# Cross attention on 97 rows: queries and keys laid out by head, column tiles for the rests, maxima among the output jobs

## The chip, the core and the metric

One NeuronCore of a Trainium2 chip. The metric is the device time of one execution in microseconds (us); lower is better. PE is TensorE, DVE is VectorE, ACT is ScalarE, POOL is GpSimd, SP is SyncE, which here only issues DMAs.

## What is computed

A decoder layer over x of [2, 2048, 512] with a context of [2, 154, 512], all in float32:

```python
x = x + linear_attention(layernorm(x))   # 16 heads of 32, elu+1 features of width 128
x = x + cross_attention(layernorm(x), ctx)
x = x + moe(layernorm(x))                # 8 experts, top 6, and a shared expert

def cross_attention(query, ctx):
    q, k, v = (proj(query, Wq, bq), proj(ctx, Wk, bk), proj(ctx, Wv, bv))   # 16 heads of 32
    scores = einsum('bhqd,bhkd->bhqk', q, k) / sqrt(32)
    attn = softmax(scores, axis=-1)                                        # over 154 keys
    return merge(einsum('bhqk,bhkd->bhqd', attn, v)) @ Wo.T + bo
```

## The kernel before

Four stages run one after another, each with its own buffers: `project`, `attend_linear`, `attend_cross` and `experts`. The 4096 tokens are cut into 8 blocks of 512 (`TB`), four a batch. Every engine has its own program; semaphores join them, and each waits in its own order, written out by hand. Products are made exact by splitting a float32 number into a high part (HI, rounded to fp32r) and a low part (LO), and adding three products, HI by HI, HI by LO and LO by HI (`PASSES`).

**`attend_linear`** works on two blocks at once: the heads of block i+1 (`heads`, `attend_group`) are laid between the output jobs of block i (`out_proj`, `transposes`, and XQ, the projection of the queries for cross attention). Four PSUM banks rotate over the jobs in the order of `JOBS`; a bank may be written again when DVE has read the job that had it (`dve_read`). At a block's end PE does XQ 0, the last group of the next heads, XQ 1 and 2, the spreads R 0 to 3 of the reciprocals (`spread_out`), and XQ 3. DVE copies each XQ with its bias to `xq` (L814), an SBUF tile for the whole block, and SP stores it to `xq_dram` with one DMA (L635) when the last is there. Ahead of that store in SP's queue stand the three loads of `q3` for the block after next (L605), for all blocks but the last two. ACT copies the next numerators after normalisation (`normalised`, L680).

**`attend_cross`** loads that block (`load_xq`, L1070), splits it on ACT and DVE (`split_xq`), and holds queries as [128 features, 512 tokens] per group of four heads. The keys `k_w` are masked: the key tile of a head is 128 rows of which 32 are not zero. Scores are made transposed, keys on the partitions: 128 keys of a head are one unit, and the remaining 26 keys of the four heads of a group are a fifth unit, so 20 units a block. A unit is three passes (L1375) and a fourth (L1380) that subtracts each query's maximum:

```python
for c, (s, m) in enumerate(PASSES):
    nc.tensor.matmul(s_bank[n % SBANKS][:], k_w[:, s, g, j * P:(j + 1) * P], q[:, m, g], start=(c == 0), stop=False)
nc.tensor.matmul(s_bank[n % SBANKS][:], minus[:, n // SU, n % SU], mxt[:], start=False, stop=True).then_inc(s_full, 1)
```

ACT takes the exponential of a unit from one of two banks to `ring` (L1156). `attend_group` sums values and denominators: four float32 passes of 32 columns for the heads' main keys (L1407, L1398) and one of 128 columns for the rests (L1409, L1400). The maxima of block k+1 come from other passes (`maxima`, L1349 and L1353), HI by HI only, queries on the partitions, reduced by DVE (L1222); they are spread over the score units of block k, and turned by `turn_maxima`. Then come the division (L1279, L1282), the spreads (L1462), the normalisation (L1287, L1163, L1291), the output projection (L1427), the sum with its statistics (L1239 to L1246), the norm (L1252) and the transposes (L1436), copied by DVE (L1259). Here three PSUM banks rotate. The two batches are a loop; at its start PE makes keys and values (L1321, L1326) and DVE masks them.

## Time and profile before

| | us |
|---|---|
| Median of 3 runs | 2907.85 |
| The runs | 2906.36 to 2916.95 |
| Span of the profiled execution | 2905.3 |
| PE busy in it | 2740.4 (94%) |
| DVE, ACT, POOL busy | 1386.4, 830.9, 133.0 |
| Mean granted clock of TensorE (1 is full) | 0.972 |

The span goes from the first to the last instruction. The profiled execution's own time is not recorded apart from its span; the runs beside it differ from the span by 1 us and more. A window row gives the busy time of each engine in a stretch of the span with its number of instructions, then the granted clock, the share of the DMA engines and the rate. In a timeline row stand the start, the length, the engine and line, and what was released by whom. Matmuls overlap one another, so what one costs is read from start to start, not from its length; a float32 pass shows as two instructions.

### The profile page before, as it was taken

Reading aid. Unit: us, or ns where it says so; the run is one execution under the profiler, and the core shown is the slowest. Engines: PE = TensorE matmul, PEld = TensorE weight load, DVE = VectorE, ACT = ScalarE, POOL = GpSimd, SP = SyncE. Lnnn points to the kernel's source line nnn. Section 1 sums busy time; section 2 is a strip of 40 time slices with the busy share of each in tenths; the row PEclk is TensorE's granted clock in tenths of the full one; section 3 lists DMA queues with packets and bytes.
Section 4 is the critical chain, followed back from the end, with each engine's and each line's share of the span. In section 5 each row is a group of like instructions: output and inputs, shape, how many; then the busy total and the mean of one; then the engine's idle time right before and its main releaser. Section 6 shows DMA issues by size and latency. Waiting matters only on the chain. (4 is left out here: it accounts for less than half of the span.)

```text
span 2905.3 us, 35331 instructions
## 1 busy us (share of the span) xinstructions
PE 2740.4 (94%) x12752; PEld 1961.9 (68%) x12752; DVE 1386.4 (48%) x2146; ACT 830.9 (29%) x1332; POOL 133.0 (5%) x101
## 2 busy tenths in 40 slices
PE   7999999889999699989997999999998999999999
PEld 5666666536556455455555888888886888888887
DVE  4444444368777455465645333333345433433333
ACT  3333333365553133223222111111222122111111
POOL 0000000011121011111110000000000000000000
PEclk9999999989999699989998999999999999999999
DMA  5111111174643311121214000000014000100001
GB/s 171 44 43 43 43 43 29 44 189 128 168 131 101 106 59 52 44 88 59 87 58 155 24 22 22 22 22 22 22 43 174 22 22 22 43 22 22 22 22 58
DMA packets 45023, 182.38 MB, mean 63 GB/s; under 512 B 4496, under 2 KB 6288, under 8 KB 33808
## 3 DMA queue, kind: packets, MB, share of 16 engines
q1 hardware_dynamic: 44656, 180.67, 19.4%
q0 software_dynamic: 288, 0.69, 0.1%
q8 instruction: 45, 0.74, 0.1%
q14 instruction: 34, 0.28, 0.0%
HBM read 123.31 MB, written 58.72 MB: 63 GB/s over the span
## 5 line engine op out<-in xcount | busy, mean ns | idle before, releaser
L1769 PE MATMUL ex_pg<-ex_x,ex_w 128*128 128x512 f32 x3840 | 885.6, 390 | 3.3 <-DVE ex_lt L1652 3.3
L1769 PEld LDWEIGHTS ex_pg<-ex_x,ex_w 128*128 128x128 f32 x3840 | 723.3, 188 | 153.9 <-issue 3.5
L1784 PE MATMUL ex_pd<-ex_w,ex_ht 128*128 128x512 f32 x1920 | 446.6, 389 | 0.0
L1718 DVE TENSOR_TENSOR ex_h<-ex_s_g,ex_pg 128x512 f32<-128x512 f32 x160 | 110.0, 688 | 648.8 <-PE ex_pg L1769 647.9
L1784 PEld LDWEIGHTS ex_pd<-ex_w,ex_ht 128*128 128x128 f32 x1920 | 360.4, 188 | 74.8
L1625 ACT ACTIVATE ex_s_g<-ex_pg 128x512 f32<-128x512 f32 x160 | 95.8, 599 | 748.6 <-PE ex_pg L1769 748.5
L1690 DVE SCALAR_TENSOR_TENSOR ex_acc<-ex_pd,ex_share,ex_acc 128x512 f32<-128x512 f32 x320 | 234.4, 748 | 90.3 <-PE ex_pd L1784 85.5
L450 PE MATMUL pr_pj<-pr_xt,pr_w 128*128 128x512 f32 x768 | 179.6, 395 | 3.1 <-DVE pr_qs L352 1.6
L450 PEld LDWEIGHTS pr_pj<-pr_xt,pr_w 128*128 128x128 f32 x768 | 145.2, 190 | 40.3 <-DVE pr_xt L342 6.8
L366 DVE SCALAR_TENSOR_TENSOR pr_kp<-pr_pk,pr_e 128x512 f32<-128x512 f32 x128 | 87.8, 691 | 142.4 <-ACT pr_e L303 108.1
L1156 ACT ACTIVATE cr_ring<-cr_s_bank 128x512 f32<-128x512 f32 x160 | 95.7, 598 | 202.5 <-PE cr_s_bank L1380 202.5
L1375 PE MATMUL cr_s_bank<-cr_xq,cr_k_w 128*128 128x512 f32 x480 | 151.7, 429 | 0.0
L1222 DVE TENSOR_REDUCE cr_mx<-cr_bank 128x4 f32<-128x512 f32 (+1 forms) x160 | 105.7, 688 | 93.8 <-PE cr_bank L1349 65.7
L1628 ACT CAST ex_ht<-ex_h 128x512 fp32r<-128x512 f32 x160 | 98.6, 616 | 181.4 <-DVE ex_h L1718 181.4
L299 ACT ACTIVATE pr_e<-pr_pk 128x512 f32<-128x512 f32 x128 | 76.4, 597 | 183.2 <-PE pr_pk L462 182.5
L462 PEld LDWEIGHTS pr_pk<-pr_f_w,pr_kt 128*128 128x128 f32 x384 | 64.6, 188 | 88.4 <-issue 72.9
L476 PE MATMUL pr_p_ks<-pr_kp,pr_ones 128*32 128x512 f32 x256 | 123.0, 592 | 0.0
L462 PE MATMUL pr_pk<-pr_f_w,pr_kt 128*128 128x512 f32 x384 | 115.4, 419 | 0.0
L1721 DVE TENSOR_TENSOR ex_ht<-ex_h,ex_ht 128x512 fp32r<-128x512 f32 x160 | 110.3, 689 | 6.8
L1427 PE MATMUL cr_bank<-cr_wo,cr_u 128*128 128x512 f32 x384 | 100.0, 407 | 5.7 <-DVE cr_u L1291 5.7
L850 PE MATMUL li_bank<-li_u_ln,li_wq 128*128 128x512 f32 x384 | 97.2, 407 | 8.4 <-DVE li_u_ln L783 8.4
L1375 PEld LDWEIGHTS cr_s_bank<-cr_xq,cr_k_w 128*128 128x128 f32 x480 | 88.5, 193 | 21.9 <-issue 7.7
(180 smaller groups left out, 2881.5 us busy)
## 6 DMA issues: line engine op xcount, KB each, us to landing
stage<-in_units SPq DMA_DIRECT2D x21, 1536.0 KB, 6.2
li_q<-q_scratch SPq DMA_DIRECT2D x21, 1024.0 KB, 12.1
q_scratch<-pr_qs SPq DMA_DIRECT2D x64, 256.0 KB, 4.0
x_scratch<-cr_x SPq DMA_DIRECT2D x16, 1024.0 KB, 4.3
pr_x<-in_x SPq DMA_DIRECT2D x8, 1024.0 KB, 5.2
li_x<-in_x SPq DMA_DIRECT2D x8, 1024.0 KB, 5.2
x_scratch<-li_x SPq DMA_DIRECT2D x8, 1024.0 KB, 3.9
xq_scratch<-li_xq SPq DMA_DIRECT2D x8, 1024.0 KB, 3.9
```

The costliest lines, as they stand in the source:

```text
L450: mm = nc.tensor.matmul(bank_of(key)[:], stationary(s, c), moving(m, c), start=(n == 0), stop=(n == C * 3 - 1))
L462: mm = nc.tensor.matmul(pk[n % 4][:], kt[:, s, g, t * P:(t + 1) * P], f_w[:, m, g], start=(q == 0), stop=(q == 2))
L476: nc.tensor.matmul(p_ks[g * HD:(g + 1) * HD, :], ones[:], kp[:, n % 4], start=(t == 0), stop=(t == TT - 1), skip_group_check=True).then_in ...
L1222: nc.vector.tensor_reduce(dst, src, AX.X, ALU.max).then_inc(dve_read, 1)
L1375: nc.tensor.matmul(s_bank[n % SBANKS][:], k_w[:, s, g, j * P:(j + 1) * P], q[:, m, g], start=(c == 0), stop=False)
L1427: mm = nc.tensor.matmul(bank_of(k, "O", t)[:], u[:, s, g, t * P:(t + 1) * P], wo[:, m, g], start=(n == 0), stop=(n == 3 * G - 1))
L1628: nc.scalar.copy(ht[:, s % 2, HI, f], h[:, f]).then_inc(ht_hi, 1)
L1690: nc.vector.scalar_tensor_tensor(acc[:, n], pd[t][:], share[:, n, bass.ds(e + s // BLK, 1)], acc[:, n], ALU.mult, ALU.add).then_inc(d_take ...
L1718: nc.vector.tensor_tensor(h[:, f], s_g[:, f], pg[2 * f + 1][:], ALU.mult).then_inc(h_set, 1)
L1721: nc.vector.tensor_tensor(ht[:, s % 2, LO, f], h[:, f], ht[:, s % 2, HI, f].bitcast(F32), ALU.subtract).then_inc(ht_lo, 1)
L1769: mm = nc.tensor.matmul(pg[2 * f + which][:], w[:, slot, sp_, col:col + P], x3[:, m, k, c * TB:(c + 1) * TB], start=(n == 0), stop=(n == 3 ...
L1784: mm = nc.tensor.matmul(pd[t][:], ht[:, s % 2, sp_, f, t * P:(t + 1) * P], w[:, slot, m, WD + f * D:WD + (f + 1) * D], start=(n == 0), sto ...
```

## The change

- In `attend_linear` the copy of XQ splits into HI on ACT (`query`) and LO on DVE; `xq` has two slots, used in turn by the four groups, and each group goes out with its own DMA (HI and LO). The scratch tensor holds both halves.
- In `attend_cross` SP loads queries by head, [32 features x 3, 512 tokens] as HI, LO, HI, one group in three DMAs, into a ring of six slots `q3`. The keys are laid out to match as HI, HI, LO, so one pass over 96 rows gives the sum of the three products. Row 97 of the queries is the maximum of the head, and that of the keys is -1, so that scores and shift are one pass of 97 rows. The rest unit of a group is four passes (`k_rest`), one a head.
- The keys get to that layout by 24 DMAs a batch (`place_keys`). The maxima are computed on 96 rows from all three products, in pieces of 154 keys, three to a bank; they are turned, copied by ACT and brought into row 97 by four DMAs on ACT's queue (`maxima_out`).
- The rests in the sums over values and in the denominators are four passes of 32 columns, column tiles like the main ones. The reciprocals are split into HI and LO, so that the spreads are fp32r.
- The maxima of the next block's first two groups lie among the output jobs of the block before, one at each place, the other two groups among the scores; the output jobs of a block come after the first sum over values of the next. The transposes' copies move to ACT. The batches are written out, and the keys and values of batch 1 stand ahead of the last output jobs of batch 0. The semaphores of this stage are not primed in a block of their own.

```diff
-        xq = sb("xq", [P, G, TB])
+        xq = sb("xq", [P, 2, 2, TB], F32R)
...
-                    sp.wait_ge(dve_read, 2 + job(i, ("XQ", G - 1)))
-                    sp.dma_start(xq_dram[i], xq[:].rearrange("p g t -> p (g t)")).then_inc(xq_out, 16)
+                    for g in range(G):
+                        sp.wait_ge(dve_read, 2 + job(i, ("XQ", g)))
+                        sp.dma_start(xq_dram[i].rearrange("s p n -> p s n")[:, :, g * TB:(g + 1) * TB],
+                                     xq[:, g % 2].bitcast(F32)).then_inc(xq_out[g % 2], 16)
...
+                def query(i, g):
+                    act.wait_ge(xq_out[g % 2], 1 + 32 * i + 16 * (g // 2))
+                    act.wait_ge(filled, 2 + job(i, ("XQ", g)))
+                    nc.scalar.activation(xq[:, g % 2, HI], bank_of(i, ("XQ", g))[:], ACT.Identity, bias=bq[:, g:g + 1])\
+                        .then_inc(xq_hi, 1)
...
+                    query(i, 0)
...
                     next_num(3)
+                    query(i, 1)
+                    query(i, 2)
                     if more:
                         normalised(i + 1)
+                    query(i, 3)
...
-                    dve.wait_ge(xq_out, 1 + 16 * i)
                     for g in range(G):
-                        dve.wait_ge(filled, 2 + job(i, ("XQ", g)))
-                        nc.vector.tensor_scalar(xq[:, g], bank_of(i, ("XQ", g))[:], bq[:, g:g + 1], None, ALU.add)\
+                        dve.wait_ge(xq_hi, 2 + G * i + g)
+                        nc.vector.scalar_tensor_tensor(xq[:, g % 2, LO], bank_of(i, ("XQ", g))[:], bq[:, g:g + 1],
+                                                       xq[:, g % 2, HI].bitcast(F32), ALU.add, ALU.subtract)\
                             .then_inc(dve_read, 1)
                         if g == 0 and more:
                             divide(i + 1)
...
+    PIECES = [[(t, j) for j in range(3)] for t in range(TT)] + [[(t, 3) for t in range(3)], [(3, 3)]]
...
+                def load_q(i, g):
+
+                    n = G * i + g
+                    if n >= QRING:
+                        sp.wait_ge(s_full, SU * (n - QRING + 1))
+                    src = xq_dram[i].rearrange("s (j d) (g t) -> s d g j t", j=HG, g=G)
+                    for r, s in enumerate((HI, LO, HI)):
+                        sp.dma_start(q3[r * HD:(r + 1) * HD, n % QRING].bitcast(F32), src[s, :, g]).then_inc(q_in[n % QRING], 16)
...
+                    for r, s in enumerate((HI, HI, LO)):
+                        rows = slice(r * HD, (r + 1) * HD)
+                        for j in range(HG):
+                            src = k_nat[j * HD:(j + 1) * HD, s].bitcast(F32)
+                            sp.dma_start(k_main[rows].rearrange("p (g j) k -> p g j k", j=HG)[:, :, j].bitcast(F32),
+                                         src[:, :, 0:KEYS]).then_inc(k_in, 16)
+                            sp.dma_start(k_rest[rows].rearrange("p (g j) k -> p g j k", j=HG)[:, :, j, j * HD:(j + 1) * HD]
+                                         .bitcast(F32), src[:, :, P:KW]).then_inc(k_in, 16)
...
+                def maxima_out(i):
+                    act.wait_ge(filled, POS[(i, "MT")] + 1)
+                    if i:
+                        act.wait_ge(mx_in, 16 * G * i)
+                    nc.scalar.copy(mxt[:], bank_of(i, "MT")[0:H, :]).then_inc(act_read, 1)
+                    act.wait_ge(act_read, ACT_AT[(i, "MT")])
+                    for g in range(G):
+                        act.dma_start(q3[K3:ROWS, slot_of(i, g)].bitcast(F32).rearrange("p j t -> p (j t)"),
+                                      mxt[g * HG:(g + 1) * HG].bitcast(F32)).then_inc(mx_in, 16)
...
+                    for i in range(first, first + BLK):
+                        more = i + 1 < first + BLK
+                        if i > first:
+                            normalised(i - 1)
+                        take_num(i, 0)
+                        if i > first:
+                            turned(i - 1)
+                        weights(i, 2)
+                        take_num(i, 1)
+                        weights(i, 3)
+                        take_num(i, 2)
+                        if more:
+                            maxima_out(i + 1)
+                        take_num(i, 3)
+                        if more:
+                            weights(i + 1, 0)
+                            weights(i + 1, 1)
...
+                def maximum(i, g, n):
+                    bank_free(i, "MX", g, n)
+                    if n == 0:
+                        q = G * i + g
+                        pe.wait_ge(q_in[q % QRING], 48 * (q // QRING + 1))
+                    if g == 0 and n == 0 and i % BLK == 0:
+                        pe.wait_ge(k_in, 16 * K_DMAS * (i // BLK + 1))
+                    for at, (t, j) in enumerate(PIECES[n]):
+                        mm = nc.tensor.matmul(bank_of(i, "MX", g, n)[:, at * KEYS:(at + 1) * KEYS],
+                                              q3[0:K3, slot_of(i, g), j, t * P:(t + 1) * P], k_main[0:K3, g * HG + j],
+                                              start=True, stop=True, skip_group_check=True)
+                    mm.then_inc(filled, 1)
+
...
+                def scores(i, g, units):
+
+                    n = SU * (G * i + g)
+                    if g == 0:
+                        pe.wait_ge(mx_in, 16 * G * (i + 1))
+                    for j in range(SU):
+                        if n + j >= SBANKS:
+                            pe.wait_ge(s_read, n + j - SBANKS + 1)
+                        out = s_bank[(n + j) % SBANKS][:]
+                        if j < HG:
+                            mm = nc.tensor.matmul(out, k_main[:, g * HG + j, 0:P], q3[:, slot_of(i, g), j], start=True,
+                                                  stop=True)
                         else:
...
+                            for h in range(HG):
+                                mm = nc.tensor.matmul(out, k_rest[:, g * HG + h], q3[:, slot_of(i, g), h], start=(h == 0),
+                                                      stop=(h == HG - 1))
+                        mm.then_inc(s_full, 1)
+                        maxima(units[j:j + 1] if j < HG else units[HG:])
...
+                def attend(i, g):
+                    n = G * i + g
+                    pe.wait_ge(s_read, SU * (n + 1))
...
+                        for j in range(HG):
+                            nc.tensor.matmul(p_den[j * HD:(j + 1) * HD, :], one_col[:, g], slot[j], start=(g == 0),
+                                             stop=False, skip_group_check=True)
+                        for j in range(HG):
+                            mm = nc.tensor.matmul(p_den[j * HD:(j + 1) * HD, :], rem_ones[:, g, j * HD:(j + 1) * HD],
+                                                  slot[HG], start=False, stop=(g == G - 1), skip_group_check=True)
...
+                def output(i, units):
+                    per = -(-len(units) // 12)
+                    take = lambda n: units[n * per:(n + 1) * per]
+                    half_way, whole = 6, 3 * G
+                    out_proj(i, 0, 0, half_way)
+                    maxima(take(0))
+                    out_proj(i, 0, half_way, whole)
+                    maxima(take(1))
...
+                    for i in range(first, first + BLK):
+                        more = i + 1 < first + BLK
+                        early = mx(i + 1, 0) + mx(i + 1, 1) if more else []
+                        if i > first:
+                            spread_out(i - 1)
+                        attend(i, 0)
+                        if i > first:
+                            output(i - 1, early)
                         else:
...
+                            maxima(early)
+                        scores(i, 2, mx(i + 1, 2) if more else [])
+                        attend(i, 1)
+                        scores(i, 3, mx(i + 1, 3) if more else [])
+                        attend(i, 2)
+                            turn_maxima(i + 1)
+                        attend(i, 3)
+                            scores(i + 1, 0, [])
+                            scores(i + 1, 1, [])
```

ACT at the end of a block of `attend_linear` (li_e: exponentials, li_num: numerators, li_u_att: normalised numerators). Before:

```order
L669 ACTIVATE li_e<-li_e 128x512
L672 REGISTER_ALU
L674 REGISTER_ALU
L675 COPY li_num<-li_p_num 128x512
L679 REGISTER_ALU
L680 CAST li_u_att<-li_num 128x512
```

And now:

```order
L694 ACTIVATE li_xq<-li_bank,li_bq 128x512
L676 REGISTER_ALU
L678 REGISTER_ALU
L679 COPY li_num<-li_p_num 128x512
L693 REGISTER_ALU
L694 ACTIVATE li_xq<-li_bank,li_bq 128x512
L692 REGISTER_ALU
L693 REGISTER_ALU
L694 ACTIVATE li_xq<-li_bank,li_bq 128x512
L683 REGISTER_ALU
L684 CAST li_u_att<-li_num 128x512
```

Four activations of the queries have come in, the third of them ahead of the four copies of the normalised numerators.

SP at the same place now, the loads of q and then the stores of the queries (`li_dve_read` is the count of jobs that DVE has read):

```order
L606 ISA [waits li_filled]
L606 DMA li_q<-q_scratch 32x8192
L606 ISA
L606 DMA li_q<-q_scratch 32x8192 x2
L636 REGISTER_ALU
L637 ISA [waits li_dve_read]
L637 DMA xq_scratch<-li_xq 128x2x512
L636 REGISTER_ALU
L637 ISA [waits li_dve_read]
L637 DMA xq_scratch<-li_xq 128x2x512
```

Where one store followed the loads, there are now four (two shown), each behind a wait of its own.

PE in a steady block of `attend_cross`, from the sum over values of a group on (cr_ring: exponentials, cr_s_bank: scores, cr_bank<-cr_k_w: maxima). Before:

```order
L1407 MATMUL cr_p_num<-cr_ring,cr_v_w 32x512 x4
L1409 MATMUL cr_p_num<-cr_ring,cr_v_rem 128x512
L1398 MATMUL cr_p_den<-cr_ring,cr_one_col 32x512 x4
L1400 MATMUL cr_p_den<-cr_ring,cr_rem_ones 128x512
L1373 REGISTER_ALU
L1375 MATMUL cr_s_bank<-cr_xq,cr_k_w 128x512 x3
L1380 MATMUL cr_s_bank<-cr_mxt,cr_minus 128x512
L1338 REGISTER_ALU
L1349 MATMUL cr_bank<-cr_k_w,cr_xq 128x512
L1373 REGISTER_ALU
```

And now, from the turned maxima of the next block to the spreads of this one:

```order
L1476 MATMUL cr_bank<-ident,cr_mxp 128x128 x4
L1507 MATMUL cr_p_den<-cr_ring,cr_one_col 32x512 x4
L1510 MATMUL cr_p_den<-cr_ring,cr_rem_ones 32x512 x4
L1519 MATMUL cr_p_num<-cr_ring,cr_v_w 32x512 x4
L1522 MATMUL cr_p_num<-cr_ring,cr_v_rem 32x512 x4
L1489 MATMUL cr_s_bank<-cr_q,cr_k_main 128x512 x4
L1493 MATMUL cr_s_bank<-cr_q,cr_k_rest 128x512 x4
L1489 MATMUL cr_s_bank<-cr_q,cr_k_main 128x512 x4
L1493 MATMUL cr_s_bank<-cr_q,cr_k_rest 128x512 x4
L1538 MATMUL cr_bank<-cr_rec,cr_spread 128x256 x16
L1519 MATMUL cr_p_num<-cr_ring,cr_v_w 32x512 x4
```

The shift passes (cr_mxt, cr_minus) are gone, three score passes have become one, the rests of a group have gone from one pass to four, and between the scores of the next block's first two groups stand no maxima.

## Rows read from the trace of the kernel before

**Rows 1.** Windows of before, by stage; columns: busy us and instructions per engine, PEclk, DMA share, GB/s

```profile
590.00:965.00 375.00, 332.40 (x1588) 207.23 (x1580) 275.69 (x477) 182.97 (x339) 60.20 (x40) 0.94 0.49 136
...
992.67:1051.54 58.87, 54.78 (x229) 29.71 (x229) 34.84 (x52) 16.19 (x25) 4.53 (x1) 0.86 0.15 54
1051.54:1111.95 60.41, 58.96 (x276) 33.48 (x277) 37.01 (x65) 18.57 (x30) 7.48 (x5) 1.00 0.19 70
1227.64:1268.90 41.26, 33.12 (x128) 23.64 (x128) 27.14 (x55) 8.51 (x14) 2.92 (x4) 0.88 0.21 79
1504.02:1526.00 21.98, 18.76 (x80) 13.52 (x80) 17.31 (x36) 2.49 (x5) 2.92 (x4) 0.97 0.12 49
```

**Rows 2.** Timeline, PE, linear stage, around a block's end; start us, length us

```profile
839.92 0.72 PE L862 MATMUL li_bank<-li_q,li_f_w 96*128 96x512 f32 x2 [1.35 <-DMA li_q<-q_scratch]
...
878.60 2.01 PE L895 MATMUL li_bank<-li_rec,li_spread 128*128 128x512 f32 x8
880.45 2.96 PE L850 MATMUL li_bank<-li_u_ln,li_wq 128*128 128x512 f32 x12
...
884.79 0.73 PE L862 MATMUL li_bank<-li_q,li_f_w 96*128 96x512 f32 x2 [1.39 <-DMA li_q<-q_scratch]
```

**Rows 3.** Timeline, DVE, the same block

```profile
871.16 0.75 DVE L814 TENSOR_SCALAR li_xq<-li_bank,li_bq 128x512 f32<-128x512 f32 x1 [1.13 <-PE li_bank L850]
...
879.55 1.27 DVE L753 TENSOR_TENSOR li_num<-li_num,li_bank 128x512 f32<-128x512 f32 x2
```

**Rows 4.** Timeline, DMA queue of SP, the same block

```profile
867.23 1.33 SPq L605 DMA_DIRECT2D li_q<-q_scratch  x3
```

**Rows 5.** The instructions of line 605, the loads of q

```profile
DMA to landing us min/median/max: 7.5/12.1/16.5
```

**Rows 6.** DMA issues; columns: count, KB each, median us to landing

```profile
li_bq<-in_bqT SPq DMA_DIRECT2D x1, 2.0 KB, 11.1
...
cr_bk<-in_bkT SPq DMA_DIRECT2D x1, 2.0 KB, 1.6
```

**Rows 7.** Timeline, PE, cross attention, first two blocks

```profile
1015.85 0.74 PE L1353 MATMUL cr_bank<-cr_k_w,cr_xq 128*128 128x128 f32 x4
1016.43 0.92 PE L1375 MATMUL cr_s_bank<-cr_xq,cr_k_w 128*128 128x512 f32 x3
...
1017.65 0.86 PE L1375 MATMUL cr_s_bank<-cr_xq,cr_k_w 128*128 128x512 f32 x3
...
1018.81 0.86 PE L1375 MATMUL cr_s_bank<-cr_xq,cr_k_w 128*128 128x512 f32 x3
...
1042.66 1.06 PE L1407 MATMUL cr_p_num<-cr_ring,cr_v_w 128*32 128x512 f32 x8
...
1046.77 1.07 PE L1398 MATMUL cr_p_den<-cr_ring,cr_one_col 128*32 128x512 f32 x8
...
1051.54 4.14 PE L1462 MATMUL cr_bank<-cr_den,cr_spread 128*128 128x256 f32 x16 [0.60 <-DVE cr_den L1282]
```

**Rows 8.** Timeline, PE, linear stage, two sets of column tiles

```profile
901.17 1.06 PE L882 MATMUL li_p_num<-li_qp,kv_w 128*32 128x512 f32 x8
...
903.02 0.66 PE L912 MATMUL li_bank<-ident,li_xn 128*128 128x128 f32 x4
```

**Rows 9.** Timeline, ACT, linear stage, two activations back to back

```profile
885.32 1.09 ACT L664 ACTIVATE li_e<-li_bank 128x512 f32<-128x512 f32 x2 [1.27 <-PE li_bank L862]
```

**Rows 10.** Timeline, DVE, cross attention

```profile
994.86 12.46 DVE L1222 TENSOR_REDUCE cr_mx<-cr_bank 128x4 f32<-128x512 f32 x20
...
1060.10 0.69 DVE L1239 TENSOR_TENSOR cr_x<-cr_x,cr_bank 128x512 f32<-128x512 f32 x1 [1.05 <-PE cr_bank L1427]
...
1061.93 0.42 DVE L1265 COPY cr_mxt<-cr_bank 128x512 bf16<-128x512 bf16 x1
```

**Rows 11.** Windows, one stretch after short passes in the linear stage

```profile
862.40:865.90 3.50, 3.50 (x16) 0.61 (x16) 1.74 (x3) 2.13 (x5) 0.00 (x0) 0.51 0.82 294
```

837 lines of the change are left out of this document (434 added, 403 removed).

## The prediction

> **What bounds the kernel now.** I read the stages first [rows 1]: the linear stage (590 to 965 us), the first stretch of cross attention, one steady block, the change of batch, and the tail. In a steady block of cross attention PE is busy for 58.96 of 60.41 us at the full clock, DVE for 37, ACT for 19. So there the length of PE's list sets the time. The linear stage is different: PE 332 of 375 us, DVE 276, and a share of 0.49 of the DMA engines. Its block ends with the queries' projection [rows 2], the copies to SBUF on DVE [rows 3], and the loads and the store of the DMA queue [rows 4, 5]: a block lasts from 839.92 to 884.79, 44.8 us, and its last wait is for the load of q, 1.39 us. The experts (from 1526 us on) are untouched and cost nothing either way. The profiled execution's span is 2905.3 us and the median of the runs 2907.85; I add 2.6 us at the end for that.
>
> **Linear stage.** Removed: one store of 1024 KB a block, and DVE's copy with bias (0.75 us, four a block). Added: four activations on ACT, about 0.6 us each (ACT idles here), four DVE operations of about the same 0.75 us, and four stores of 512 KB. By itself that costs nothing. But the output tile xq now has two slots for four groups. ACT's query 2 may run only when the store of query 0 has landed, and by the program's order the three loads of q for the block after next stand ahead of it in SP's queue. The times of one block: loads issued at 867.23, 0.44 us apart [rows 4], landing 7.5, 12.1 and 16.5 us after their issues [rows 5], so the last at 868.1 + 16.5 = 884.6. The loads land one after another, 4.5 us apart. A transfer behind them waits for them: the 2 KB of bq took 11.1 us behind the first q loads, the 2 KB of bk 1.6 us with nothing ahead [rows 6]. Query 0 is read at 871.16 + 0.75 [rows 3], with ACT's step 0.8 later; its store goes out at 872.8 and has 512 KB, half of the 4.4 us by which a load of 1024 KB follows the one ahead. It lands at 884.6 + 2.2 = 886.8.
>
> The Trainium skill, "DMA: Bandwidth & Descriptors" (Queues, rings and completion order), says that an engine starts the descriptors of one ring in order, and that a semaphore's increment comes after all earlier writes of that DMA engine. By that rule the trace agrees with a small transfer that takes 11.1 us.
>
> Until then ACT stands in front of query 2, with the four copies of the next heads' numerators queued behind it, and DVE in front of its second half, with the normalisation behind it (now at 879.55 [rows 3]). PE has issued spreads R0 to R2 by 880.1; R3 takes the bank of query 2. New times: query 2 on ACT to 887.4, on DVE to 888.2, then R3; XQ3 needs the bank of R0, read at 888.9, against 880.45 now [rows 2]; it ends at 891.8. The next block's heads then start at 891.8 and ACT, after the last query, takes them up at 893.3, against 885.3 now. The 1.39 us wait for q is gone and inside this. I take 8 us a block; 6.9 is what PE's own queue gives, 9.6 if XQ3 runs at half clock after the gap. Six of the eight blocks still have a q load ahead (the last two load nothing): **+48 us**, ends +20 (if part of the store overtakes the loads) and +60.
>
> **Cross attention, a steady block on PE.** Prices are start to start.
> - Scores: 60 passes and 20 shifts go, 32 passes of 512 columns come. One unit of three passes, shift and one maxima pass takes 1018.81 - 1017.65 = 1.16 us [rows 7], 0.232 a pass. 80 x 0.232 = 18.6 becomes 32 x 0.232 = 7.4.
> - Maxima: 16 passes of 512 and 16 of 128 (5.3 us) become 64 of 154 columns. Four of 128 take 1016.43 - 1015.85 = 0.58, 0.145 each; in proportion to 512 columns 154 would be 0.07. I take 0.11, nearer the short pass: 7.0 us (4.5 to 14.8).
> - Attention over values: 4.11 us a group with one full float32 pass for the rest per product (1042.66 to 1046.77 [rows 7]). The linear stage's two sets of four column tiles take 903.02 - 901.17 = 1.85 us [rows 8], so four sets 3.7: 16.4 becomes 14.8.
> - Spreads: 4.2 us [rows 7] becomes 2.0, by the eight fp32r passes of 512 columns that take 1.85 us (878.60 to 880.45 [rows 2]), here 16 of 256.
> - Output projection (11.4), transposes (1.5) and turned maxima (0.4) stay.
>
> Sum on PE: 7.4 + 7.0 + 14.8 + 2.0 + 13.3 = 44.5 us, against about 58. **But the block will not be 44.5 us long**, since the other engines no longer hide:
> - Scores of groups 0 and 1 have no maxima between them. A unit is 0.23 us for PE, while with two banks ACT takes 0.6 us for one exponential and a hand-over; two in 1.09 us where nothing stands between them, so 0.49 a unit at best and 0.55 with the hand-over [rows 9]. With the rest's four passes a group takes 3.3 us, not 1.9: +2.8. Groups 2 and 3: +0.7.
> - The maxima now travel by PE transpose, ACT copy, four DMAs issued by ACT and then 8 KB each: 0.6 + 4 x 0.44 + 1.6 (the issue by SP's row, the landing by the bk row) is about 4.2 us, behind it one attend of 3.7: +0.7. Were a row transfer to stand behind loads, 11.1 would be the bound.
> - Output: one projection, two maxima and one transpose is 3.4 us of PE. DVE needs 1.8 for the sum and its statistics (1060.10 to 1061.93), 2 x 0.62 for the maxima [rows 10], 0.5 for the norm, 3.6 in all, in an order in which the fourth projection waits for the bank of maxima 5, behind the third sum: +2.0; the others, and the last norm's transposes, +3.
> - Normalisation, partly behind an attend: +0.5.
>
> 44.5 + 9.7 = 54.2 us against 60.4, -6.2 in each of six block periods: **-37 us**.
>
> Costed at nothing: the q loads (12 of 256 KB a block for one of 1024 KB; 12 x 0.44 = 5.3 us of SP, and a DMA share of 0.19 now [rows 1]; each is issued some 30 us before its first pass, behind waits for score units that are then done); the transposes' copies, which go from DVE to an idle ACT; the split of xq on DVE, which goes. Without that cover (SP held by a store) a late q load would stop PE at the maxima, 4 us.
>
> **The ends of the batches.** Before: 58.9 to the first spread (twice), 41.3 from a batch's last spread to the next maxima, 22.0 for the tail [rows 1]. The first maxima stay bound by DVE (20 reduces in 12.46 us [rows 10]; now 24 shorter ones, about 13). Batch 0 has 12 early maxima with no output job to hide in (7 us). At the change of batch DVE does the keys and values first and the division (3.4 us of reciprocal and 3 around it) after them, so PE waits some 5 us, then 4 in the normalisation; in exchange the 24 maxima lie among the output jobs. Laid end to end I get 172.6 where now there are 170.9: +2. Before the first maxima the keys are placed by 24 DMAs, 24 x 0.44 = 10.6 us of SP and 2 to land, after 983 us; they end at 996 against 992.7 now: **+3**. Without a row for small descriptors in SBUF this is 0 to +15; in batch 1 it lies behind the context and the division.
>
> **Clock.** Where PE does little, the granted clock falls: 1.2 GHz from 862.40 to 865.90 (0.51 in the row [rows 11]) after a stretch of short passes with waits, and 0.86 over the first 58.9 us of cross attention [rows 1]. The changed block has three such stretches (the two groups of scores, the fourth projection, the last transposes). A stretch of 3.5 us at half clock costs up to 1.7 us if PE is then the bound, nothing if DVE is; I take 2 us for each of eight blocks: **+16**, ends 0 and +40.
>
> Sum: 48 - 37 + 2 + 3 + 16 = +32 on 2905.3; with the 2.6 us, **2940 us**. A measurement of this kernel tells 0.5%, 14.5 us, from no change.
>
> A rule that would give more for the column tiles: the Trainium skill, "TensorEngine Tiling (Array Packing)" (Key Properties), says that a change of tiling mode drains the engine. The old order changes mode four times in a group, the new one twice. The rows leave room for 0.4 us a group in all, which the sum has.
>
> **Rivals.**
> - *The store is not held* (chance 0.13). If the transfers shared the DMA engines, the store would land by 878.6, when query 2 is ready, and the linear stage would cost nothing: 2940 - 48 = 2892, faster. For it: the stores are spread over all engines and the loads have large descriptors. Against: the three loads land one by one, and the 11.1 us of bq.
> - *PE's sum decides in cross attention too* (0.07): the stalls shrink to the 3 us a block of today, 47.5 us a block, -77 instead of -37, the clock holds: 2940 - 40 - 16 = 2884. Against: one ACT exponential of 0.6 us per 0.23 us of PE.
> - *Gain and loss meet* (0.20): the linear wait costs 40, the clock falls half as often, and the blocks gain 8 each: 2907 + 40 - 48 + 5 + 8 is about 2912.
> - *Everything waits longer* (0.18): half clock after each gap (9.6 us a block, 58) and in cross attention (+35), with the row DMAs landing 2 us later: 58 - 37 + 5 + 35 + 16 = +77, 2985. It decides when ACT's four issues and the landing take over 5 us.
> - Forecast as worked out (0.42): 2922 to 2958.
>
> Chances: faster 0.20, within 0.5% 0.20, slower 0.60. The range of 8 in 10 goes from 2888 to 2975, since it has to take in the held and the gained time in their worst pairing.
>
> **What would show it.** In the changed profile: DVE's wait for query 2, and ACT's for the DMA of xq, 8 us in six blocks; a linear period near 53 us. In cross attention a period near 54 us; PE waits for ACT's exponentials in the scores without maxima, below 2 us for the maxima's rows; projections waiting for DVE. More slices of PEclk below 9. The forecast is wrong if the linear period stays at 45 us (first rival), or if the steady block is under 49 or over 60 us.

## The result and the profile after

| | before | changed |
|---|---|---|
| Median (4 runs each, same chip), us | 2912.3 | 2994.67 |
| The runs, us | 2906.36 to 2916.95 | 2989.54 to 3009.11 |
| Span of the profiled execution, us | 2905.3 | 3007.0 |
| PE busy, us | 2740.4 (94%) | 2722.3 (91%) |
| Mean granted clock | 0.972 | 0.934 |

The ratio is 1.029, 95% interval 1.026 to 1.032: slower, by 82 us where 32 were forecast, and above the range. The profiled execution is the slowest of the changed kernel's four, and that of the kernel before lies below its median; the decomposition below is of these two spans, which differ by 101.7 us, some 19 us more than the medians.

The page of the changed kernel, busy tenths in 40 slices. Cross attention is in the 14th to the 22nd; PEclk has a 9 in one of these nine.

```profile
PE   7999999778788569988886999999999999999999
...
PEclk9999999889899758887897999999999999999999
DMA  4111111364544343423323100010013200000001
```

Windows of the changed kernel that answer to [rows 1]: linear stage, first stretch of cross attention, the block after it, a steady block of the second batch, the change of batch. (Columns as in [rows 1].)

```profile
590.00:1012.00 422.00, 343.30 (x1588) 218.36 (x1580) 276.26 (x478) 205.11 (x373) 60.81 (x41) 0.89 0.49 141
1073.40:1146.42 73.02, 63.71 (x313) 41.62 (x314) 32.01 (x55) 19.87 (x35) 4.53 (x1) 0.69 0.37 90
1146.42:1210.25 63.83, 57.94 (x310) 37.10 (x308) 32.63 (x63) 18.93 (x33) 6.75 (x5) 0.82 0.35 101
1440.76:1498.26 57.50, 51.27 (x309) 32.67 (x308) 32.41 (x63) 18.92 (x33) 6.76 (x5) 0.95 0.39 110
1332.85:1376.61 43.76, 33.45 (x140) 27.31 (x141) 28.02 (x58) 4.22 (x7) 2.20 (x4) 0.73 0.12 36
```

PE is busy for fewer us than before in a steady block, 51.3 against 59.0, but the first stretch (73.0 us against 58.9) and the clock (0.69 against 0.86) give it back. Laid against the trace of before, the difference of the two spans is (behind the last row the two agree to 0.1 us):

| Stretch | forecast | measured |
|---|---|---|
| Linear stage, to the start of the last block's query projection | +48 | +47.3 |
| from there to the first maxima (47.4 us before, 80.8 now) | +3 | +33.4 |
| first maxima to the experts' router (545.8 before, 564.3 now) | -19 | +18.5 |
| router to the first expert product | 0 | +2.6 |

**Linear stage.** ACT and PE at one block's end, timelines of the changed kernel. Query 2 is the activation at 873.36, and the last of the four spreads (its two passes) waits behind it:

```profile
863.32 0.69 ACT L694 ACTIVATE li_xq<-li_bank,li_bq 128x512 fp32r<-128x512 f32 x1 [3.16 <-PE li_bank L865]
873.36 0.69 ACT L694 ACTIVATE li_xq<-li_bank,li_bq 128x512 fp32r<-128x512 f32 x1 [9.35 <-DMA xq_scratch<-li_xq]
...
874.88 1.22 PE L910 MATMUL li_bank<-li_rec,li_spread 128*128 128x512 f32 x2 [7.42 <-DVE li_xq L828]
```

Over the stage, in the groups of ACT's line 694, its wait for the stores is 55.7 us, six of 9.3:

```profile
L694 ACT ACTIVATE li_xq<-li_bank,li_bq 128x512 fp32r<-128x512 f32 x32 | 22.0, 688 | 115.3 <-PE li_bank L865 59.6 <-DMA xq_scratch<-li_xq 55.7
```

**Start of cross attention**, timelines of POOL and PE. GpSimd waits 40.95 us for the two loads of constants, then come its copies (to 1056.5), the placing of the keys (to 1072), the maxima:

```profile
1052.27 1.89 POOL L1195 CAST cr_k_rest<-cr_ring 97x2048 fp32r<-97x2048 f32 x1 [40.95 <-DMA cr_ring<-in_minus_row]
1054.22 2.24 POOL L1197 CAST cr_k_main<-cr_ring 1x2464 fp32r<-1x2464 f32 x1
...
1073.40 14.39 PE L1463 MATMUL cr_bank<-cr_k_main,cr_q 96*128 96x154 f32 x64 [44.06 <-DMA cr_k_rest<-stage]
```

**A steady block**, timeline of PE in the second batch, from the turned maxima to the spreads:

```profile
1485.21 0.66 PE L1476 MATMUL cr_bank<-ident,cr_mxp 128*128 128x128 f32 x4
...
1490.23 0.73 PE L1489 MATMUL cr_s_bank<-cr_q,cr_k_main 97*128 97x512 f32 x2 [0.79 <-DMA cr_q<-cr_mxt]
1491.47 0.99 PE L1489 MATMUL cr_s_bank<-cr_q,cr_k_main 97*128 97x512 f32 x2 [0.51 <-ACT cr_ring L1230]
1492.66 1.21 PE L1493 MATMUL cr_s_bank<-cr_q,cr_k_rest 97*128 97x512 f32 x4 [0.20 <-ACT cr_ring L1230]
...
1496.39 2.07 PE L1493 MATMUL cr_s_bank<-cr_q,cr_k_rest 97*128 97x512 f32 x4
1498.26 3.94 PE L1538 MATMUL cr_bank<-cr_rec,cr_spread 128*128 128x256 f32 x16
```

The waits for the rows (0.79) and for the exponentials (0.5 and less) are there and have the size that was forecast. But the four rest passes take 1.0 us at 1492.66 and 1.9 at 1496.39, and the spreads 3.9 instead of 2.0: the clock fell between the two, after short passes with waits.

### The profile page after: what moved, and what is told of

Read it like the earlier page. It is cut to its first block and busy times, and to the rows that moved or that the text cites. A ratio compares the mean times of both kernels' runs of the same rounds, so it can differ in the third digit from the quotient of the medians.

```text
span 3007.0 us, 34993 instructions
## 1 busy us (share of the span) xinstructions
PE 2722.3 (91%) x13008; PEld 1987.3 (66%) x13008; DVE 1340.3 (45%) x2117; ACT 848.5 (28%) x1388; POOL 131.0 (4%) x102
## 5 line engine op out<-in xcount | busy, mean ns | idle before, releaser
L1326 DVE TENSOR_REDUCE cr_mxp<-cr_bank 128x3 f32<-128x462 f32 x192 | 105.6, 582 | 171.2 <-PE cr_bank L1463 170.5
L1463 PE MATMUL cr_bank<-cr_k_main,cr_q 96*128 96x154 f32 x512 | 94.7, 316 | 51.4 <-DMA cr_k_rest<-stage 44.1
L1463 PEld LDWEIGHTS cr_bank<-cr_k_main,cr_q 96*128 96x128 f32 x512 | 94.5, 237 | 66.5 <-issue 46.5
L1561 PE MATMUL cr_bank<-cr_wo,cr_u 128*128 128x512 f32 x384 | 106.6, 424 | 18.7 <-DVE cr_mxp L1326 11.7
L865 PE MATMUL li_bank<-li_u_ln,li_wq 128*128 128x512 f32 x384 | 108.2, 441 | 8.4 <-DVE li_u_ln L798 8.4
```

The source lines that it names most:

```text
L865: mm = nc.tensor.matmul(out, stationary(s), moving(m), start=(c == 0 and n == 0), stop=(c == C - 1 and n == 2))
L1326: nc.vector.tensor_reduce(dst.rearrange("p t j -> p (t j)") if t == t_end else dst[:, :, 0], src, AX.X, ALU.max).then_inc(dve_read, 1)
L1463: mm = nc.tensor.matmul(bank_of(i, "MX", g, n)[:, at * KEYS:(at + 1) * KEYS], q3[0:K3, slot_of(i, g), j, t * P:(t + 1) * P], k_main[0:K3, ...
L1561: mm = nc.tensor.matmul(bank_of(i, "O", t)[:], u[:, s, g, t * P:(t + 1) * P], wo[:, m, g], start=(n == 0), stop=(n == 3 * G - 1))
```

## The experiments

Ratios are to the kernel before in runs on the same chip, with the 95% interval; in percent of some 2909 us. Runs of different rows are compared by their ratios, since several chips were used. Two things were to be settled: whether the 47 and the 33 us come from where the trace puts them, and why cross attention lost.

| Run | median, us | ratio |
|---|---|---|
| the change | 2994.67 | 1.0293 (1.0262 to 1.0324) |
| e1_rest96 | 2971.03 | 1.0220 (1.0202 to 1.0239) |
| e2_four_slots | 2951.77 | 1.0158 (1.0134 to 1.0183) |
| e3_both | 2922.14 | 1.0068 (1.0040 to 1.0095) |
| e4_stores_on_act_queue | 3011.02 | 1.0357 (1.0340 to 1.0375) |
| e5_keys_two_queues | 2923.14 | 1.0045 (1.0029 to 1.0062) |
| e6_scores_twice | 2928.53 | 1.0066 (1.0043 to 1.0088) |
| e7_filled_start | 2924.26 | 1.0064 (1.0040 to 1.0089) |
| e8_loads_by_group | 2925.09 | 1.0056 (1.0038 to 1.0073) |
| e9_maxima_moved | 2920.65 | 1.0030 (1.0019 to 1.0041) |
| e10_all | 2914.98 | 1.0021 (1.0010 to 1.0031) |
| e11_before_loads_by_group | 2892.85 | 0.9941 (0.9925 to 0.9958) |
| e12_last_transposes_later | 2897.36 | 0.9959 (0.9945 to 0.9973) |
| e13_and_filled_start | 2898.34 | 0.9965 (0.9950 to 0.9981) |
| e14_fewer_row_transfers | 2903.19 | 0.9989 (0.9974 to 1.0005) |
| e15_gaps_filled | 2888.54 | 0.9932 (0.9916 to 0.9949) |
| e16_before_gaps_filled | 2890.47 | 0.9940 (0.9923 to 0.9956) |
| e17_maxima_turned_earlier | 2888.86 | 0.9929 (0.9905 to 0.9953) |
| e18_batch_starts_filled | 2872.48 | 0.9864 (0.9841 to 0.9887) |

### The load of 97 rows

```diff
-sp.dma_start(rest_raw, a["k_rest"]).then_inc(raw_in, 16)
+sp.dma_start(rest_raw[0:K3], a["k_rest"][0:K3]).then_inc(raw_in, 16)
+sp.dma_start(rest_raw[K3:ROWS], a["k_rest"][K3:ROWS]).then_inc(raw_in, 16)
```

> The load of the key remainders (97 rows of 8 KB) is made two loads: 96 rows, and the last row alone. The changed kernel has 80.8 us from the last query job of the linear stage to the first maxima, the kernel before 47.4. Theory: the 97-row transfer lands some 30 us late since it goes at some 26 GB/s, as one stream; the split load is spread over the DMA engines, GpSimd's copy of the remainders starts 25 to 35 us earlier, and the total falls by 25 to 35 us. Rival: the 24 key-placing transfers and GpSimd's copies behind the key projections set the start; then the copy starts earlier but the maxima start at most 5 us earlier. The linear stage keeps its 47 us loss in either case.

Measured: 0.7% faster by the ratios, some 21 us. GpSimd's copy, in its timeline, starts 28 us earlier, and PE's first maxima 25.5 us (1047.9 for 1073.4). The linear stage is as in the change:

```profile
1024.28 1.89 POOL L1196 CAST cr_k_rest<-cr_ring 97x2048 fp32r<-97x2048 f32 x1 [12.97 <-DMA cr_ring<-in_minus_row]
```

The same 776 KB, with the small row behind them, take some 39 us as one transfer of 97 rows (20 GB/s) and some 11 us as two; the form alone costs 28 us. The trace of the change has a stretch in which nothing but this transfer moves data, 20 packets of one row each (window; the last columns are clock, DMA share, GB/s). A share of 0.06 of 16 engines is one engine:

```profile
1017.00:1023.00 6.00, 6.00 (x29) 5.69 (x28) 1.22 (x4) 1.58 (x4) 0.00 (x0) 0.69 0.06 27
```

The Trainium skill, "DMA: Bandwidth & Descriptors" (Why a DMA increments its semaphore by 16 and not by 1), has the rule that a transfer runs on the largest number of engines, at most 16, that divides the slowest dimension of both its sides. 97 is prime, so by the rule it is one engine, and 96 rows get 16. The traces agree with it, by the share of 0.06 and by 20 GB/s against some 70; the prediction did not apply it.

### Slots, queues and loads in the linear stage

Four slots (e2), both together (e3), the stores in another queue (e4), and the loads in pieces (e8, with two slots and the split load):

```diff
-xq = sb("xq", [P, 2, 2, TB], F32R)
+xq = sb("xq", [P, G, 2, TB], F32R)                     # e2, e3
-    sp.dma_start(xq_dram[i]..., xq[:, g % 2]...)       # e4
+    act.dma_start(xq_dram[i]..., xq[:, g % 2]...)
-sp.wait_ge(filled, 2 + job(i, ("QP", H - 1)))          # e8
-load_q(i + 2)
+sp.wait_ge(filled, 2 + job(i, ("QP", HG * g + HG - 1)))
+load_q(i + 2, g)
```

> The output tile of the queries' projection in the linear stage gets four slots for its four groups in place of two (room for it: the raw spread matrix lies in the normalised tile, the denominator's reciprocal is taken in place). Theory: the added time of the linear stage (47.3 us between the ends of the two kernels' last query jobs) is ACT's wait for the store of query 0, which lands behind the three loads of q; with four slots nothing waits for a store of the same block, the block period returns from 52 to 54 us to 45 and the total falls by 42 to 50 us. Rival: the stores' form (four of 512 KB instead of one of 1024 KB) and the added split on ACT and DVE are what costs; then at least 25 of the 47 us stay.

> Four slots and the split load together. If the two causes are separate the gains add: 2995 - 47 - 30 = about 2918, within 0.5% of the kernel before (2912). If the start of cross attention is hidden behind something that the linear stage's end sets (the units overlap), the two together give less than the sum by 10 us or more. What then stands against the kernel before is the effect of cross attention's new order by itself: the trace says +19 us less what half clock in the first blocks costs.

> Two slots as in the change, but the four stores of the queries are issued by ACT, not by SP, so they stand in another DMA queue than the three loads of q. Theory (a store waits because it is behind the loads in its queue): the store of query 0 lands within 4 us of its issue, ACT's wait for it falls from some 8 us a block to under 2, and the total falls by 35 to 47 us. Rival (the store waits for DMA engines that the loads keep busy, whichever queue it is in): the wait stays above 5 us a block and the total falls by under 15 us.

> Two slots as in the change, split load of the remainders (2971), and in the linear stage the three loads of q are cut into four groups of heads, each issued as soon as the four heads' passes are done, so that most of the 3 MB is in before the store of query 0 is issued. Stores on another queue did not shorten the wait for query 0's store (54 us over six blocks, as with SP's queue). Theory after that: the store waits for DMA engines that hold the loads' data in flight, not for its place in the queue; with the loads spread over the block it lands within some 5 us, ACT's wait falls below 15 us over six blocks, and the total falls by 40 to 55 us to 2916 to 2931, without any slot more. Rival (a store from these two slots takes 9 us for a reason of its own, such as its many descriptors): the wait stays over 40 us.

Measured, by the ratios: e2 takes 1.35% away (39 us), e3 2.25% (65 us), against 39 + 21, so the gains add. The block period (from spread to spread, steady blocks), 51.4 to 53.3 us in the change and 43.1 to 44.9 before, is 43.3 to 44.9 in e2. e4 goes against the theory: ACT's wait for the store is as long from its own queue, and ACT, which now also waits for DVE before each issue, makes the block 52 to 55 us. The group of ACT's queries in e4:

```profile
L690 ACT ACTIVATE li_xq<-li_bank,li_bq 128x512 fp32r<-128x512 f32 x32 | 22.0, 688 | 114.0 <-PE li_bank L870 56.6 <-DMA xq_scratch<-li_xq 54.3 <-PE li_bank L915 3.0
```

So it is not the place in the queue. In the change the DMA engines are all busy when the store is issued (window of the changed kernel; the last columns are clock, DMA share, GB/s):

```profile
860.00:870.00 10.00, 7.47 (x34) 5.55 (x30) 5.83 (x5) 0.85 (x2) 0.00 (x0) 1.00 1.01 210
```

e8 confirms it from the other side: with the loads issued over the whole block the store finds free engines, the wait is gone with two slots (the landing is 5.0 us at most, 13.5 in the change), and the time falls by 1.6% against e1, 46 us:

```profile
L702 ACT ACTIVATE li_xq<-li_bank,li_bq 128x512 fp32r<-128x512 f32 x32 | 22.0, 686 | 63.2 <-PE li_bank L873 63.2
```

The same cut in the kernel before:

> The kernel before, with the loads of q in the linear stage cut into four groups of heads, issued as the passes of each group are done. There the block ends with a wait for q of 1.39 us. Theory: the wait goes in six blocks, the total falls by 5 to 9 us (0.2 to 0.3%). Rival: the queues' engines are as busy as before in the stretch of the XQ jobs (x is loaded there too) and nothing changes, or twelve issues a block instead of three hold up SP's other transfers: same or 3 us slower. It also says whether the gain of the same cut in the changed kernel comes from the load itself or from the store that no longer waits.

It gains 17 us, twice the expectation. The matmuls' waits for q go from 19.4 us (9 times) to 10.9 (twice, both at the stage's start), and the period, 44.3 to 44.9 in most blocks, is 41.6 in four and 43.2 in two: more than the 1.39 of the wait. What more there is comes with the clock: the column tiles that ran at 0.51 in the kernel before [rows 11] run at full clock in e11 (below).

### The start of cross attention

```diff
-sp.dma_start(rest_raw, a["k_rest"])                    # all rows, copied by GpSimd
+sp.dma_start(rest_raw[K3:ROWS], a["k_rest"][K3:ROWS])  # e5: last row; zeros from the cleared maxima tile
-place_keys(sp, b)                                      # 24 transfers
+place_keys(sp, b, main=True); place_keys(act, b, main=False)   # 12 and 12
```

> Four slots in the linear stage as before; at the start of cross attention GpSimd makes the zeros of the key remainders from the cleared maxima tile instead of copying a loaded constant, only the last rows are loaded, and the 24 key-placing transfers are issued by SP (12) and ACT (12) side by side. With four slots and the split load alone (2922) the maxima start at 1002.9, 39.9 us after the last query job's copy began, the 24 issues take 19 us of it, and GpSimd's two copies hold them until 983.8 though the split keys are ready at 978.8. Theory: the start is a chain of split keys, issues, landing; it becomes 979 + 12 x 0.65 + 2 = about 989, so the total falls by 11 to 16 us to about 2908. Rival: the transfers themselves (many small descriptors) bound it, not their issue; then two queues gain under 6 us.

> Four slots and split load (2922), and PE executes 70 passes of 512 columns, whose result nobody reads, while it would wait for the placed keys at the start of cross attention. Theory (the clock is what is lost there: the 64 maxima passes and the scores after them run at half clock, 14.4 us for the 64 passes instead of 7): the 64 passes take 7 to 8 us, though DVE's 24 reduces then set 13, and the clock of the first 60 us rises from about 0.6 to over 0.8; the total falls by 5 to 15 us. Rival: the first stretch is bound by DVE and by the rows' transfers; the clock rises and the total stays within 3 us.

e5: the maxima start at 992.9 instead of 1002.9, but of that 4 us come from a linear stage that ended earlier (last query copy at 957.8, not 962.1); the ratio says 0.2%, which is not clear of noise. The issues are done at 983.3 (timelines of the two queues), and PE's wait ends 9.6 us after that: in the change, from one queue, these transfers land 1.8 to 2.1 us after their issue (medians), here, from two at once, 6.1 to 6.6. The rival was right in this part.

```profile
974.26 8.41 ACTq L1116 DMA_DIRECT2D cr_k_rest<-stage  x12
975.00 8.28 SPq L1113 DMA_DIRECT2D cr_k_main<-stage  x11
```

e7: the 64 maxima passes still take 13.8 us (14.4), the clock of the first 64 us rises from 0.64 to 0.68 only, the total does not change. DVE's reduces set those 13 us, and the 5.1 us wait for the rows behind them lets the clock fall again.

### Cross attention: the clock or the waits

e6 issues each head's scores twice where no maxima lie between them. e9 puts the next block's maxima of group 0 there:

```diff
-early = mx(i + 1, 0) + mx(i + 1, 1)                    # e9
+early = mx(i + 1, 1)
-    scores(i + 1, 1, [])
+    scores(i + 1, 1, mx(i + 2, 0))
```

> Four slots and split load (2922), and in the scores that have no maxima between them (groups 0 and 1, and groups 2 and 3 of the batches' last blocks) each head's pass is issued twice, with the same result: more work for PE, no new wait for anyone. Theory (the granted clock falls there because PE waits for ACT between short passes, and the four rest passes and the spreads after them then run at half clock, 3.9 us instead of 2.0): the clock holds, each block loses 2 to 4 us in spite of 8 more passes, and the total falls by 10 to 30 us. Rival (PE's own work counts): 8 blocks x 8 passes x 0.22 is 14 us more on PE, of which what lies in the waits for ACT is free; the total stays or rises by up to 14 us and the spreads stay at 3.9 us.

> Four slots and split load (2922); in cross attention the maxima of the next block's group 0 go from the output jobs into the scores of group 1 (that had none between them), and group 1's six units take single places around the output jobs 0, 1 and 3. Nothing is computed more or less. Theory: the steady block of 57.5 us holds two avoidable losses: the output part, 22.2 us for 16 us of PE work, waits for DVE's reduces (0.5 to 1.7 us each), and the scores without maxima let the granted clock fall, with the spreads behind them at half clock; with the move the output part takes 18 us, the spreads 2 to 3, the block 51 to 53, and the total falls by 25 to 45 us, below the kernel before. Rival: DVE's division (6.4 us beside the same scores) delays the moved reduces, three banks are full and PE stops there as long as it saved: block 56 to 58, total within 8 us of 2922.

> Everything together: two slots with loads by group in the linear stage, keys placed from two queues with the zeros made on the chip, and the moved maxima. If the gains are separate: what the moved maxima give (25 to 45) and 7 to 10 more from the start on 2922, that is 2870 to 2890, 0.8 to 1.3% below the kernel before. If the move alone gives nothing: about 2915.

e6: the spreads' passes have a median of 280 ns instead of 415, and ACT's exponentials hold PE for 4.0 us instead of 10.0, so the clock does hold there; 80 more passes eat it up, and the total is the same. e9: 0.4% faster, some 11 us, where 25 to 45 us were expected. Its timeline and windows show why. The spreads begin at full clock, but the last transposes wait for their norm, and 14 us behind them run at 0.63:

```profile
1414.00 0.43 PE L1550 MATMUL cr_bank<-cr_rec,cr_spread 128*128 128x256 f32 x2
1414.79 1.44 PE L1550 MATMUL cr_bank<-cr_rec,cr_spread 128*128 128x256 f32 x10 [0.35 <-DVE cr_mxp L1336]
...
1438.96 1.08 PE L1582 MATMUL cr_bank<-ident,cr_xn 128*128 128x128 f32 x4 [1.84 <-DVE cr_xn L1386]
```

```profile
1414.00:1435.50 21.50, 19.88 (x117) 14.25 (x117) 15.74 (x33) 3.93 (x7) 1.65 (x3) 1.00 0.22 46
1435.50:1449.50 14.00, 11.89 (x54) 8.44 (x56) 5.97 (x13) 4.64 (x8) 1.75 (x2) 0.63 0.76 291
```

The half clock went from one gap to the next. e10 puts e8's loads, e5's keys and e9's order together: 0.5% below e3, where the three by themselves add up to 0.7%. e12 takes that gap away by order (the last transposes behind the scores of group 2), e14 the number of row transfers alone:

```diff
-for g in range(G):                                     # e14: runs of slots, 1 or 2 transfers
-    act.dma_start(q3[K3:ROWS, slot_of(i, g)]..., mxt[g * HG:(g + 1) * HG]...)
+for g, n in row_runs(i):
+    act.dma_start(q3[K3:ROWS, to:to + n]..., mxt[g * HG:(g + n) * HG]...)
 scores(i, 2, mx(i + 1, 2))                             # e12, besides
+transposes(i - 1, 3)
```

> Everything together (2915) with the maxima's rows alone changed: one or two transfers a block instead of four. ACT issues each in 0.58 us, so the last row lands 1.7 us earlier. Theory: PE's wait for them falls from 18.3 us (eight waits, the longest 8.3) to 7 to 12, and the total by 5 to 12 us. Rival: one larger transfer into one partition takes longer to land than four in a row (8 KB each, into the same partition), so the wait stays at 15 us or more and the total within 3 us.

> On top of everything together (2915): the last transposes of an output part go behind the scores of group 2, so that PE does not wait for their norm, and the maxima's rows go by one or two transfers a block instead of four. Theory (the clock falls at every gap of more than a microsecond after short passes, and what is lost is not the gap but the half clock after it): the six gaps of 1.84 us go, and with them some 14 us at a granted clock of 0.63 each; 4 to 7 us a block, 25 to 40 in all, plus 5 to 10 for the rows: total 2870 to 2885. Rival (waits count one by one): 6 x 1.84 + 8 = 19, about 2896. Second rival: the clock falls elsewhere instead, total over 2905.

> The same with 30 passes of 512 columns that nobody reads, in the wait for the placed keys at the start of cross attention. The first 60 us of cross attention run at half clock otherwise. Theory: 5 to 10 us less than without them. Rival: DVE's reduces and the rows' transfers set that stretch, within 3 us.

e14 gains 0.3%: the waits for rows are 12.7 us, not 18.3, but the longest stays at 8.6. e12 gains 0.3% more, together 18 us: near the number of the rival that counts the waits one by one (19), and short of the 30 to 50 of the theory. It is near the number only, since the waits were traded: from e14 to e12 those for the transposes' norm fall from 15.1 to 3.0 us, those for the rows rise from 12.7 to 22.0. The four steady blocks are no shorter in e12's trace (228.9 us against 226.2, spread to spread); the last block of each batch and the change between them are (197.2 against 207.9). The half clock is not a constant price behind every gap. e13, with 30 passes at the start, changes nothing, like e7.

**The clock by itself.** The linear stage has one place where both kernels run the same passes with the same two waits. In e11 (first line) it stays at full clock, in e12 (second line) not, and the periods are 41.6 and 44.4 us:

```profile
851.80 1.07 PE L890 MATMUL li_p_num<-li_qp,kv_w 128*32 128x512 f32 x8 [0.18 <-DVE li_qp L742]
```

```profile
863.06 1.93 PE L905 MATMUL li_p_num<-li_qp,kv_w 128*32 128x512 f32 x8 [0.18 <-DVE li_qp L757]
```

```diff
+for _ in range(3 if h in (12, 15) else 0):
+    nc.tensor.matmul(bank_ahead(i, ("QP", h))[:], f_w[:, h], q3[:, h], start=True, stop=True)
```

> The version with the last transposes later (2897), and in the linear stage the passes of heads 12 and 15 are issued four times each with the same result, 0.22 us a pass, in front of the two gaps of 0.84 and 1.01 us in which PE waits for DVE. Theory (the clock, not the wait, is what is lost): the clock stays at 1.00 through the block, the period falls from 44.4 to 41.6 us in most of seven blocks, and the total falls by 12 to 20 us to about 2880. Rival (the period is set by DVE's or ACT's chain, the half clock lies beside it): the gaps stay as long as they are, the period stays at 44.4, the total within 3 us; if the passes are not hidden, up to 9 us slower.

> The kernel before with loads by group (2893), with the same repeated passes. Its periods are 41.6 us in five blocks and 43.1 in two, so less is left to gain. Theory: 0 to 5 us faster, or the same. Rival: the passes cost 1.3 us a block, 9 us slower.

The same stretch in e15, timeline and window (e12's window of the same stretch stands behind it):

```profile
856.76 0.50 PE L887 MATMUL li_bank<-li_q,li_f_w 96*128 96x512 f32 x1 [0.17 <-DVE li_qp L757]
857.43 1.07 PE L907 MATMUL li_p_num<-li_qp,kv_w 128*32 128x512 f32 x8 [0.17 <-DVE li_qp L757]
```

```profile
855.00:861.00 6.00, 5.66 (x34) 2.77 (x33) 4.38 (x8) 5.49 (x11) 0.00 (x0) 1.00 0.91 239
```

```profile
862.00:868.00 6.00, 5.04 (x23) 1.48 (x23) 3.02 (x6) 4.04 (x9) 0.00 (x0) 0.72 0.98 282
```

The six periods behind the first are all 42.8 us where e12 has 44.4, and the total falls by 9 us (the intervals just overlap, but the last spread of the stage starts 8.7 us earlier in the trace, 914.8 for 923.5): passes that nobody needs made a kernel faster. The expected size (12 to 20 us) was too large, since the period did not fall to 41.6. Without the passes the gap costs the clock in some executions only: e10 and e14, with the same linear stage as e12, have periods of 42.8 in the first blocks and of 44.5 in the last four. With them no block lost it. In e16 the same six periods are 41.6, and the total is the same within its interval, as expected of a kernel that had little to gain.

Last, the row wait and the batches' starts:

```diff
-attend(i, 2); turn_maxima(i + 1)                       # e17
+attend(i, 2, between=i + 1)                            # turned between its two halves
+for _ in range(24):                                    # e18, before a batch's first scores; 40 at the start
+    nc.tensor.matmul(s_bank[1][:], wo[:, HI, 0, 0:P], wo[:, HI, 0], start=True, stop=True)
```

> The version with the gaps filled (2888.5) and one thing more: the maxima are turned between the two halves of the attention over group 2, not after it, so their rows have 1.8 us more to arrive behind PE's work. The rows' waits are 22 us in all, 8.4 at most, some 1 to 2.4 us in each of five steady blocks. Theory (a gap costs itself and the half clock after it, seen where the spreads take 3.8 us instead of 2): the five waits nearly go, 5 to 9 us, and where the clock then holds 2 to 4 us more a block: total 2868 to 2880. Rival: only the waits go, 2880 to 2884; or PE now waits for DVE's last reduce before the turn, and nothing is won.

> The same, with 40 passes in the wait for the placed keys and 24 passes in front of each batch's first scores (where PE waits 5 and 8 us for the maxima's rows), all of 512 columns, read by nobody. Theory: in the first 60 us after each batch's start the granted clock is 0.5 for some 30 us; with it held, 5 to 15 us less than without. Rival: at a batch's start DVE (24 reduces, the division) and the transfers set the pace, so the clock rises and the time stays within 4 us.

e17 wins nothing: the rows' waits go from 21.9 to 19.9 us. e18 is 0.65% faster than e17, 16 to 19 us, and 1.4% faster than the kernel before (1.1 to 1.6). Against e11, the kernel before with its loads in pieces, it is 0.8%: that much is the new cross attention with all that was mended and filled in it. The first 65 us and the change of batch, windows of e17 and then of e18:

```profile
985.00:1050.00 65.00, 57.72 (x312) 39.10 (x313) 32.68 (x56) 18.14 (x33) 4.54 (x1) 0.72 0.37 86
1255.00:1305.00 50.00, 39.85 (x193) 26.92 (x193) 19.05 (x39) 12.96 (x23) 5.10 (x2) 0.66 0.39 111
```

```profile
985.00:1050.00 65.00, 59.34 (x342) 41.93 (x343) 33.33 (x58) 19.09 (x34) 4.54 (x1) 0.84 0.40 93
1255.00:1305.00 50.00, 45.82 (x232) 30.71 (x236) 19.53 (x39) 14.98 (x26) 5.12 (x2) 0.80 0.38 113
```

Here the fill works and in e7 and e13 it did not. What is new are the passes after the maxima, where PE waits 5 to 8 us for rows and has its own scores behind them; they were not run without the 40 at the start.

**What cross attention gained and lost.** Windows from the first maxima to the router: before, then the change, e3, e12 and e18, each from its own trace.

```profile
992.67:1538.46 545.79, 505.01 (x2256) 288.06 (x2256) 307.85 (x533) 154.59 (x243) 59.89 (x41) 0.95 0.18 68
```

```profile
1073.40:1637.66 564.26, 476.73 (x2512) 302.71 (x2512) 266.83 (x515) 156.21 (x272) 54.27 (x41) 0.81 0.33 94
```

```profile
1002.91:1556.28 553.37, 465.70 (x2512) 294.07 (x2513) 266.53 (x515) 155.91 (x272) 54.37 (x41) 0.84 0.33 96
```

```profile
995.56:1527.12 531.56, 458.33 (x2513) 297.19 (x2513) 268.01 (x515) 156.76 (x272) 54.17 (x41) 0.83 0.35 99
```

```profile
988.07:1508.28 520.21, 457.45 (x2561) 299.72 (x2561) 267.82 (x515) 156.14 (x272) 54.22 (x41) 0.87 0.35 101
```

Length times clock is the length as if all had run at full clock: 518 before, 457 in the change, 465 in e3. By this measure the new order saves some 54 to 61 us, and the part lost to the clock goes from 27 us (545.8 x 0.05) to 89 in e3 (553.4 x 0.16) and 107 in the change. It is an upper bound on what the clock costs, since a wait is no longer at half clock; where fill alone raised the clock (e18 against e17, 0.84 to 0.87) the stretch became 8 us shorter where the bound says some 17. These two profiled executions differ by 7 us in all and the medians by 16, so between half of the bound and nearly all of it is real there.

The same code also differs from trace to trace by what the clock does: the change, e1, e2, e3, e4 and e8 have one and the same cross attention, and it takes 564.3, 553.2, 559.8, 553.4, 564.2 and 563.9 us at a clock of 0.81 to 0.84. Before, e11 and e16 take 545.8, 546.2 and 545.8. So up to 11 of the +18.5 us in the table above lie with the execution that was profiled and not with the order.

## Why the prediction was wrong

The two spans differ by 101.7 us where +32 was forecast. Of the 70 us between them 30 lie in the start, 37 in cross attention and 3 behind the router.

- **Linear stage, +48: right in size, in part for a wrong reason.** Measured +47.3, with DVE, ACT and PE queued as told (the store's landing, 14.0 us after its issue by the forecast, took up to 13.5), and e2 and e8 take it back. The cause named was SP's queue, where the store stands behind the loads. e4 refutes it: in ACT's queue the wait is 54.3 us as against 55.7. The store waits on DMA engines that the loads keep full (share 1.01), and the rival "the store is not held" was wrong to take shared engines for free ones.

  Of the Trainium skill's rule ("DMA: Bandwidth & Descriptors", Queues, rings and completion order) the half on descriptors of one ring does not decide here. The other half, that an increment comes after all earlier writes of its DMA engine, is said there to hold across queues, and e4 agrees with that.
- **Start, +3: the step that failed first.** It measured +33.4. The key-placing transfers were priced and given 0 to +15, and the loads that initialise their target, 776 KB in a form of 97 rows, were not priced: no term has the two loads of constants or GpSimd's two copies. e1 puts 21 to 24 us of it on that one load. The rest is the 24 issues at 0.64 us, not 0.44 (15.5 us, not 10.6), and the 4.1 us of copies.
- **Steady blocks, -37: the waits were right, and at full clock the work is about as forecast.** Scores without maxima, the fourth projection (1.7 us in e3) and the rows (0.79) are as written; the path of the rows was added up as 4.2 us where its terms give 4.0. The spreads were mis-sized by the clock: 3.9 us, not 2.0. For the periods, 56.2 us were forecast with the clock's 2 us in it: 57.5 and 58.8 in the second batch, but 62.6 and 63.8 in the first, at a clock of 0.85 and 0.82 (57.5 at a clock of 0.95 is 54.6 at full clock, against 54.2). Together the six block periods went from 352.2 to 347.5 us, 336.2 in e3, where -37 and 12 of the clock's 16 were forecast.
- **Clock, +16: the term that failed in size.** Ends 0 and +40 were given; the measured bound is some +61 in e3 (89 less 27) and +80 in the change (107 less 27). e18's fill tests 17 us of it, at the batches' starts, and shows 8 to 16 to be real; for the rest it is a bound. I priced the falls in the steady blocks and left out the first 70 us of each batch, where 0.69 stands for the 0.86 of before.
- **Ends of the batches, +2:** first maxima to first spread is 73.0 us for 58.9, +14, and from the last spread of batch 0 to the first of batch 1 it is 107.9 for 100.3, +8. Most of the +14 is this half clock and 5.1 us for the first rows, whose latency nothing hides there (0.7 was taken for a steady block and carried over).
- The rival "everything waits longer" (2985, chance 0.18) came nearest; the point from which it decides, rows landing after 5 us, is met at the batches' starts only.

Open: why the same gap costs the clock in one block and not in another, and where e12's last 0.3% come from.
